# Pair, image and weight writes issued from ScalarE's queue, with several planned places changed

## The reference

```python
h = jnp.maximum(_layernorm(x), 0.0)
x = x + relu(dinv[:, None] * (adj + I) * dinv[None, :] @ h @ W0)        # layer 0, dinv = (deg + 1) ** -0.5
x = x + (dis[:, None] * adj * dis[None, :]) @ h @ W1.T + b1             # layer 1
x = x + relu(norm(adj + I) @ h @ W2)                                    # layer 2
# layer 3, two branches on the same adj
e = where(adj != 0, exp(-leaky_relu(s_left[:, None] + s_right[None, :])), 0)
x = x + sigmoid(attn_a * (e / (sum(e) + 1e-5)) @ (h @ W_sa) + attn_b * (adj @ (h @ W_gcnb) + b_gcnb))
```

## Time and profile before

| | us |
|---|---|
| median of 3 runs | 1831.3 |
| the 3 runs | 1825.85, 1831.3, 1831.81 |
| profiled execution | 1827.36 |
| its span | 1825.6 |
| PE busy in the span | 1709.7 |
| mean granted clock of PE | 0.982 |

### The profile page before, as it was taken

The page is one execution under the profiler, slowest core; times in us unless marked ns, Lnnn a source line. Parts: engine busy times, 40 slices in busy tenths (PEclk is TensorE's granted clock), DMA queues, the critical chain, the costliest instruction groups (busy, mean ns, idle before and its releaser), DMA issues.

```text
span 1825.6 us, 31726 instructions
## 1 busy us (share of the span) xinstructions
PE 1709.7 (94%) x12862; PEld 1167.5 (64%) x12862; DVE 1130.1 (62%) x1957; ACT 773.4 (42%) x1178; POOL 610.2 (33%) x567
## 2 busy tenths in 40 slices
PE   3999887898898999899999999999999899999996
PEld 1444333655776878768877888887888544444453
DVE  5777996856757666543434443454641667888865
ACT  5675554544434443322312232210110567768654
POOL 0001754435656553512312121111210445445431
PEclk9999999999999999999999999999999999999999
DMA  9984897797777787986575798767644443444423
GB/s 394 360 305 157 275 269 262 246 322 283 258 252 272 263 296 253 326 301 225 162 249 185 226 319 302 282 212 241 223 145 165 141 130 91 151 129 119 145 80 124
DMA packets 185559, 417.08 MB, mean 228 GB/s; under 512 B 18340, under 2 KB 79136, under 8 KB 181680
## 3 DMA queue, kind: packets, MB, share of 16 engines
q1 hardware_dynamic: 185412, 415.04, 66.4%
HBM read 303.80 MB, written 111.17 MB: 227 GB/s over the span
## 4 chain that ended last, share of the span: by engine, by line
PE 66%; DVE 17%; DMA 6%; ACT 5%; issue 3%; POOL 2%; SPq 1%; ACTq 0%; DVEq 0%; POOLq 0%
PE ps L1123 13%; PE ps L1168 10%; PE ps L1170 10%; PE ps L1169 10%; PE ps L1215 6%; PE ps L1217 6%; PE ps L1216 6%; DVE U L1468 6%; DMA U<-in_adjT 3%; DMA Ad<-U 2%; DVE stage L1451 1%; ACT U L1797 1%; DVE CT L1507 1%; DMA U<-in_adj 1%; DVE HB L1468 1%
## 5 line engine op out<-in xcount | busy, mean ns | idle before, releaser
L1168 PE MATMUL ps<-U,HB 128*128 128x256 f16 (+2 forms) x2520 | 636.9, 261 | 15.3 <-ACT CT L1802 6.7
L1169 PE MATMUL ps<-U,HB 128*128 128x256 f16 (+2 forms) x2520 | 636.8, 261 | 0.0
L1170 PE MATMUL ps<-U,HB 128*128 128x256 f16 (+2 forms) x2520 | 636.6, 261 | 0.0
L1215 PE MATMUL ps<-U,HB 128*128 128x512 f16 (+3 forms) x960 | 341.7, 359 | 32.6 <-DVE U L1468 18.7
L1216 PE MATMUL ps<-U,HB 128*128 128x512 f16 (+3 forms) x960 | 341.1, 358 | 0.0
L1217 PE MATMUL ps<-U,HB 128*128 128x512 f16 (+3 forms) x960 | 341.1, 358 | 0.0
L1468 DVE SCALAR_TENSOR_TENSOR U<-U,cS 128x512 f16<-128x512 f32 (+6 forms) x255 | 257.8, 1033 | 123.7 <-ACT U L1797 123.3
L1123 PE MATMUL ps<-W,OT 128*128 128x512 f16 (+1 forms) x1320 | 302.2, 383 | 17.0 <-DVE xr L1537 10.3
L1168 PEld LDWEIGHTS ps<-U,HB 128*128 128x128 f16 x2520 | 247.2, 98 | 45.4 <-DVE U L1468 7.4
L1797 ACT ACTIVATE U<-U,cS 128x512 f16<-128x512 f32 (+6 forms) x255 | 197.7, 803 | 169.4 <-POOL U L1975 47.8
L1169 PEld LDWEIGHTS ps<-U,HB 128*128 128x128 f16 x2520 | 247.4, 98 | 26.4 <-issue 0.3
(11 more groups left out here) (204 smaller groups left out, 1961.6 us busy)
## 6 DMA issues: line engine op xcount, KB each, us to landing
U<-Ad SPq DMA_DIRECT2D x83, 896.0 KB, 6.4
U<-in_adjT SPq DMA_DIRECT2D x289, 256.0 KB, 4.2
Ad<-U SPq DMA_DIRECT2D x35, 896.0 KB, 5.8
xd<-xr SPq DMA_DIRECT2D x84, 256.0 KB, 5.4
xr<-xd SPq DMA_DIRECT2D x84, 256.0 KB, 5.4
U<-in_adj SPq DMA_DIRECT2D x14, 1354.0 KB, 8.6
U<-Ad SPq DMA_DIRECT2D x23, 707.0 KB, 5.9
HBd<-stage SPq DMA_DIRECT2D x16, 896.0 KB, 7.6
```

Of the source, the lines that this page charges most:

```text
L1168: eng.matmul(o, h[0], hi, start=J == 0 and a == 0, stop=False)
L1169: eng.matmul(o, h[0], lo, start=False, stop=False)
L1170: last = eng.matmul(o, h[1], hi, start=False, stop=to in "acg" and J == 9 and a == 1)
L1215: eng.matmul(o, h[0], hi, start=j == 0, stop=False)
```

## The change

The writes of pairs (`a_keep`), images and weights (`w_keep`) are issued by ScalarE instead of SyncE, with the same waits. Places in the list change: masks, scores and splits of pass 4 get shorter leads; raw rows of chunk 12 a longer one; images are planned 16 us after the norm instead of 12; pairs 4 and 5 of h are read back at the first steps of the next pass; the pair of the two tiles of chunk 5 of a pass (t = 17) doesn't start before step 1 of the next pass; the seven stages of weights 3, 1 and 2 get other steps (the numbers are steps after the start of chunk g); the writes of pairs made ahead come 17 us after their fetch instead of 20, and 15 for the last two.

```diff
@@ -277,12 +277,12 @@
 
     def ahead(u):
         nonlocal fetched, eyed, split, summed, scored, masked
-        while scored < len(scores) and near(scores[scored], u, 6, 17) and scored < masked + 2:
+        while scored < len(scores) and near(scores[scored], u, 6, 15) and scored < masked + 2:
             if not have(("row_out", scores[scored][1]), *free_of("sc_a")):
                 break
             put("score", *scores[scored][1:])
             scored += 1
-        while masked < scored and near(scores[masked], u, 5, 15) and masked < s.count.get("split_e", 0) + 3:
+        while masked < scored and near(scores[masked], u, 5, 12) and masked < s.count.get("split_e", 0) + 3:
             if not have(("fetch",) + scores[masked], *free_of("em")):
                 break
             put("mask", *scores[masked][1:])
@@ -298,7 +298,7 @@
                 break
             put("eye", *eyes[eyed][1:])
             eyed += 1
-        while split < len(splits) and near(splits[split], u, LA, 12 if splits[split][1] >= GE else 9.6):
+        while split < len(splits) and near(splits[split], u, LA, 10.4 if splits[split][1] >= GE else 9.6):
             g, j = splits[split][1:]
             if not have(("fetch", "agg", g, j)) or splits[split] in eyes and not have(("eye", g, j)) or g < 2 and not have(("scale", g)) or g >= GE and not have(("mask", g, j)):
                 break
@@ -309,7 +309,7 @@
                 break
             put("split_e" if g >= GE else "split", g, j)
             split += 1
-        while fetched < len(SEQ) and (fetched <= u + 9 or near(SEQ[fetched], u, 9, 20)):
+        while fetched < len(SEQ) and (fetched <= u + 9 or near(SEQ[fetched], u, 9, 28 if SEQ[fetched][1] == 12 else 20)):
             g, j = SEQ[fetched][1:]
             if winograd(g) and not fly(g, j):
                 if j != whole(j):
@@ -354,7 +354,7 @@
         steps = [(0, "normed", l, 2 * J), (0.6, "normed", l, 2 * J + 1), (1.4, "h_sums", l, J), (5, "hi", l, J),
                  (6.5, "lo", l, J)]
         if J < 8 or l == 3 and J < 10:
-            steps.append((12, "image", l, J))
+            steps.append((16, "image", l, J))
         if l == 1:
             steps += [(5, "xbias", 2 * J), (5, "xbias", 2 * J + 1)]
         steps += [(9, "x_keep", "post", l - 1, 2 * J), (9, "x_keep", "post", l - 1, 2 * J + 1)]
@@ -365,7 +365,7 @@
             plan(v, *stage)
         quiet = later(u, 8 if J >= 7 else 12)
         if J < 8:
-            gone = AT["agg", 6 * l - 1, 2 * J + 2] if J < 6 else AT["agg", 6 * l, 4 * J - 20]
+            gone = AT["agg", 6 * l - 1, 2 * J + 2] if J < 4 else AT["agg", 6 * l, (1, 2, 4, 8)[J - 4]]
             if l > 1:
                 plan(max(later(u, 24), gone), "restore", l, J, 0, 7)
             else:
@@ -381,7 +381,7 @@
             return
         plan(later(v, 1.3), "moments", p + 1, t)
         if t % 2:
-            plan(later(v, 2.6), "pair", p + 1, t // 2)
+            plan(max(later(v, 2.6), AT["agg", 6 * p + 6, 1] if t == 17 else 0), "pair", p + 1, t // 2)
 
     def run(kind, *a):
         if kind == "norms":
@@ -493,9 +493,9 @@
     for d, kind in enumerate(("gate_max", "gate_top", "gate_w")):
         plan(AT["agg", 2, 3] + d, kind)
     weights(4, 2, 4, 7, 12, 13, 16, 18, 24)
-    weights(3, 2, 21, 24, 31, 32, 35, 37, 43)
-    weights(1, 3, 14, 17, 20, 21, 24, 26, 32)
-    weights(2, 4, 6, 9, 15, 16, 19, 21, 27)
+    weights(3, 2, 21, 25, 29, 30, 32, 33, 40)
+    weights(1, 3, 14, 17, 20, 21, 23, 25, 29)
+    weights(2, 4, 4, 10, 18, 18, 20, 22, 26)
     for n in range(8):
         plan(AT["agg", 2, 13] + n, "v_dot", n // 4, n % 4)
     plan(AT["agg", 3, 4], "v_keep")
@@ -506,7 +506,7 @@
     for n, (g, j) in enumerate(AHEAD):
         u = later(AT["agg", 2, 1], 7.8 * n)
         for us, *stage in ((0, "fetch", "pre", g, j), (0, "fetch", "pre", g, j + 1), (7.5, "sums", g, j),
-                           (11, "split", g, j), (12, "split", g, j + 1), (20 if n < 16 else 15, "a_keep", g, j)):
+                           (11, "split", g, j), (12, "split", g, j + 1), (17, "a_keep", g, j)):
             plan(later(u, us), *stage)
     for _, g, j in SEQ:
         if GW <= g < 12 and j == whole(j) and fly(g, j):
@@ -1019,18 +1019,6 @@
                             sync.wait_ge(s_mask, s("mask", past, j))
                         for o in (0, 32, 64):
                             eng.dma_start(ft[o:o + TR, g % 2, 0:w], adjT[j * P:N, i0:i0 + w]).then_inc(s_ft[g % 2], 16)
-                elif kind == "a_keep":
-                    g, j = of
-                    sync.wait_ge(s_slo, s("split", g, j + 1 if j < 20 else j))
-                    o = lying(PLACE["pre", g, j], 14 * half(g)) if made_ahead(g, j) else kept_of(g, j)
-                    eng.dma_start(home(g, j), o).then_inc(KEPT[g, j][0], 16)
-                elif kind == "image":
-                    l, J = of
-                    sync.wait_ge(s_plo, s("lo", l, J))
-                    n = image_no(l, J)
-                    a, b = (0 if J < 8 else H21), (8 if l == 3 else 7)
-                    eng.dma_start(HBd[l][a:b, :, J, :, :].rearrange("s p h n -> p s (h n)"),
-                                  stage[:, n % 2, a:b, :, :].rearrange("p s h n -> p s (h n)")).then_inc(s_kept[n % 2], 16)
                 elif kind == "restore":
                     l, J, a, b = of
                     for at_kept in images_kept(image_no(l, J) + 1):
@@ -1057,10 +1045,6 @@
                     if k == 3:
                         sync.wait_ge(s_vdot, 8)
                     eng.dma_start(wtmp[:, :, :], (w0, w1t, w2, wg, wsa)[n].rearrange("(c p) n -> p c n", p=P)).then_inc(s_w, 16)
-                elif kind == "w_keep":
-                    n, = of
-                    sync.wait_ge(s_wlo, s("w_lo", n))
-                    eng.dma_start(Wd[n], Wp).then_inc(s_wkept, 16)
                 elif kind == "w_load":
                     n, = of
                     sync.wait_ge(s_wkept, 64)
@@ -1795,6 +1779,22 @@
                         if (g - 2, j) in KEPT:
                             act.wait_ge(*KEPT[g - 2, j])
                     eng.mul(split_of(g, j)[0], unsplit(g, j), cS[0:r, n:n + 1]).then_inc(s_shi, 1)
+                elif kind == "a_keep":
+                    g, j = of
+                    act.wait_ge(s_slo, s("split", g, j + 1 if j < 20 else j))
+                    o = lying(PLACE["pre", g, j], 14 * half(g)) if made_ahead(g, j) else kept_of(g, j)
+                    eng.dma_start(home(g, j), o).then_inc(KEPT[g, j][0], 16)
+                elif kind == "image":
+                    l, J = of
+                    act.wait_ge(s_plo, s("lo", l, J))
+                    n = image_no(l, J)
+                    a, b = (0 if J < 8 else H21), (8 if l == 3 else 7)
+                    eng.dma_start(HBd[l][a:b, :, J, :, :].rearrange("s p h n -> p s (h n)"),
+                                  stage[:, n % 2, a:b, :, :].rearrange("p s h n -> p s (h n)")).then_inc(s_kept[n % 2], 16)
+                elif kind == "w_keep":
+                    n, = of
+                    act.wait_ge(s_wlo, s("w_lo", n))
+                    eng.dma_start(Wd[n], Wp).then_inc(s_wkept, 16)
                 elif kind == "gather":
                     g, = of
                     act.wait_ge(s_agg, s("agg", g, 19))
```

## The result

| | before | after |
|---|---|---|
| median, us | 1831.55 (4 runs, 1825.85 to 1831.98) | 1802.32 (4 runs, 1798.75 to 1804.94) |
| ratio | | 0.9846, 95% interval 0.9820 to 0.9872 |
| span of the profiled execution | 1825.6 | 1799.5 |

The change makes the kernel 1.5% faster, 28 us by the ratio. The sum of the prediction was 28.5.

What follows compares the result with a forecast made beforehand. PE was taken as the bound, busy 1709.7 of 1825.6 us, with gains only in its idle or half-clock time. Terms of 35.5 less 7 for ScalarE gave 28.5 us: forecast 1801, own range 1790 to 1810, outer range 1783 to 1825.

Steps and rivals of the forecast that it cites:

- Weights: Near 300 us, fetching weight 1 earlier removes PE's 6.13 us hole and the slow clock behind it: 7 us, ends 2 and 9.5.
- Images off SyncE: At 436.59 us, raw rows no longer wait behind an image on SyncE, closing PE's 3.20 us hole: 5 us, ends 0 and 6.6.
- the holes near 584, 731 and 742: PE's holes behind writes on SyncE (575 to 589) and a fetch awaiting a pair write (731, 741): 2 us plus 2.
- Pair writes near 700: A write issued some 5 us earlier on ScalarE removes PE's 4.21 us hole at 703.86: 6.5 us, ends 0 and 7.6.
- Two queues, the same 16 engines: Rival: writes sent earlier land no earlier because reads run beside them; about 1814 us; both partial rivals together 0.25.
- The hole at 773: PE's 6.75 us wait for the gather until 779.09 goes by earlier write and later pair 8: 9 us, low end 3.4.
- Restores, raw rows, +17 us: Later restores of pairs 4 and 5, group 12's raw rows and pair writes at +17 us: 0, ends -3 and +3.
- The clock behind a hole: After some PE holes the clock is 0.51 for 6.9 us, so 3.4 us more are lost on top.
- Leads of layer 3: Near 1428 us, shorter leads cut PE's 4.2 and 1.5 us waits and a clock dip: 4 us, ends 0 and 9.
- ScalarE pays: The 102 added issues take 44 us on ScalarE, of which 7 us were charged as loss; ends 0 and 44.
- The slower rival: Rival: in groups 6 to 11 issuing writes makes ScalarE late for just-in-time splits; near 1848 us, chance 0.11.

Runs made afterwards that it cites:

- e3: The kernel before with only the seven stages of weights 3, 1 and 2 at their new steps; 1821.0 us, ratio 0.9962.
- e1: The kernel before with pair, image and weight writes issued by ScalarE, all planned places as before; 1824.6 us, ratio 0.9976.
- e2: The kernel after with pair, image and weight writes issued by SyncE again, all new places kept; 1809.1 us, ratio 0.9894.
- e6: The kernel after with one write, that of pair (11, 6), moved behind the split of step 12; 1796.7 us, ratio 0.9819.
- e11: The kernel after with write (11, 6) moved behind the split of step 12 and writes (10, 12) to (10, 18) two steps earlier; 1796.1 us, ratio 0.9818.
- e8: The kernel after with only the pair writes issued by SyncE again; 1807.1 us, ratio 0.9879.
- e10: The kernel after with the writes of images and weights issued by SyncE again, pair writes still on ScalarE; 1802.9 us, ratio 0.9855.
- e7: The kernel after with 102 more DMAs of 512 bytes on ScalarE, one just ahead of each write; 1806.8 us, ratio 0.9875.
- e4: The kernel before with only the pair writes issued by ScalarE, all places as before; 1827.2 us, ratio 0.9991.

## Why the prediction was right, and where it wasn't

The total was right, and so was what bounds the kernel: PE's holes ahead of 786 us and at 1428, and nothing between (the line of 561 us moved in no kernel). Step by step:

- **Weights, 7 us: right,** 7.0 in e3. The stall of SyncE at the fetch was the cause, and the trace after shows the fetch out 13 us earlier.
- **Images off SyncE, 5 us: the hole was read rightly and the edit wrongly.** It closes by the queue alone and by the new places alone (e1, e2: 6.2 us each). I costed only the queue and passed over the move from 12 to 16 us, which was in the diff and is the likely one of the places. Of the 4 us for the holes near 584, 731 and 742, the first gave 2 us, the other two (2.0 and 2.1 us) turned into one of 6.9.
- **Pair writes near 700, 6.5 us: came back.** The hole closed, as did ScalarE's waits. The prediction named GpSimd's sum, 7 us ahead, as what is late next, and that was the wrong place: next late was the same write as seen from SyncE (the fetch of the ready pair, 4.2 us), and the raw rows that another write overtakes (6.9 us). From (8,11) to (11,11) the kernel after is 4.0 us longer than before; with one write moved it is 3.0 shorter. So in chunk 11 the rival "Two queues, the same 16 engines" held. The Trainium skill says in "DMA: Bandwidth & Descriptors", section "Issuing engines are not separate DMA queues", that DMAs interleave on the same engines whoever issues them, and that issuing from several saves only the issuer's time. The first half is borne out by e6 (six fetches 3.6 us sooner in the middle without a write between them) and e11 (2.2 us earlier out, 0.7 earlier landed). The second half leaves out what this kernel gained by: with a queue of its own a write no longer stands behind another's wait. The queue of the pair writes is worth 4.7 us in (8,11) to (11,0) (e8 against the kernel after), where one of their waits was 9.4 us long.
- **The hole at 773, 9 us: the size right** (8.6), the cause shared wrongly. The queue alone does nothing for it (0.3 us); the delay of pair 8, the read back of pairs 4 and 5 and one of the two queue moves (pair writes, or images and weights: e8 and e10 both have the 8.6) do it together.
- **Restores, raw rows, +17 us, at 0 with ends -3 and +3: too small.** Undoing the three costs 8 us by the times; 4.6 us are the read back at the end of the pass, and the raw rows' lead shows nothing. I had looked only at how full the DMAs are. I take it that the reads stood next to the fetches of the next chunk, which this kernel needs within a few microseconds; that is read from their places, and no run shows which fetch they held up.
- **The clock behind a hole, 3.4 us each: mis-sized.** The low stretch of 6.9 us begins ahead of the hole's end, and half of it was taken as lost. PE works in it for 5.25 us, in the three others for 5.61, 4.64 and 4.51, so the loss is half of that, 2.3 to 2.8 us. The upper ends of weights, images, pair writes and the hole at 773 are then 8.7, 6.0, 6.5 and 9.7 instead of 9.5, 6.6, 7.6 and 10.8, and the 6.5 taken for the pair writes was all that there was.
- **Leads of layer 3, 4 us: 2.2.** The holes went from 4.2 to 2.2 and from 1.5 to 0.8, and the half clock stayed (0.51 for 6.9 us from 1406.6). All ten kernels with the new leads show 1.5 to 2.4 in that line, the three without 0.4 faster to 0.9 slower.
- **ScalarE pays 7 of 44 us: likely 1 to 4.** 41.4 us of issue, 2.4 by e7's rate; in (4,0) to (6,0) the kernel after is 1.0 longer than e2, and in the old order e1 is 3.9 longer than before. These 3.9 come with the images and weights, since e4, with the pair writes alone, is 1.1 shorter; that they are ScalarE's time is argued. The slower rival never came near.

So what bounds the kernel was read rightly, but that the sum came within 1 us was luck: a gain that came back (6.5 and 2 us) and one that either of two edits brings (images) were made good by edits that I had at nothing (8 us) and by a cost of ScalarE that was smaller than feared.

## What to carry to other kernels

When writes leave a queue, they no longer stand behind the reads there, and that had set a part of their order. Plan each of them for the queue it goes to: as early as the next user needs it, but behind the reads that are due first. Before costing a move to another queue, ask if a later place in the same queue closes the same hole, and cost every edit near a hole as a share of that hole, not by itself.

## What the runs showed of the hardware

Issuing a pair write takes ScalarE's queue 0.33 us at the median, where it took SyncE's 0.43, and 33.1 of ScalarE's 41.4 us of issues ran beside one of its own instructions. With a small DMA of 512 bytes put ahead of each, the same issue took 0.60 us. Writes of 0.9 MB landed sooner from ScalarE's queue, 4.7 us against 5.8 in the middle, and images later, 9.6 against 7.6 (page before and page after; here the one of after). Part of that could be their new places, but e2, with the same places and all writes on SyncE, has 5.7 and 7.4. With only the images on ScalarE (e8) they take 8.2 us.

```profile
Ad<-U ACTq DMA_DIRECT2D x35, 896.0 KB, 4.7
...
HBd<-stage ACTq DMA_DIRECT2D x16, 896.0 KB, 9.6
```
